# Six weight transposes of the first batch by DMA instead of TensorE, 512-key score matmuls, and new instruction orders in a post-norm decoder layer

## What is computed

```python
def attn(X):                                  # B=4, S=512, D=512, 16 heads
    Q, K, V = (X @ Wq.T + bq) * s, (X @ Wk.T + bk) * s, X @ Wv.T + bv
    scores = where(causal, einsum('bqhd,bkhd->bhqk', Q, K), -inf)
    return einsum('bhqk,bkhd->bqhd', softmax(scores), V) @ Wo.T + bo
def xattn(logits, ctx):                       # ctx: 4 x 512 x 256
    energy = (ctx @ Wxq.T + bxq) @ (ctx @ Wxk.T + bxk).T
    return einsum('bln,bmn->blm', logits, softmax(energy))
def ffn(x):
    xq = activation_quant(rms_norm(x))
    return (silu(xq @ sign(Wg).T) * (xq @ sign(Wu).T)) @ sign(Wd).T
x = layernorm(x + attn(x)); x = layernorm(x + xattn(x, ctx)); x = layernorm(x + ffn(x))
```

## Time and profile before

| | |
|---|---|
| median of 3 runs | 603.66 us (601.66 to 605.85) |
| the profiled execution | 603.64 us |
| its span from first to last instruction | 601.8 us |
| PE busy with matmuls | 562.8 us, 94% |
| DVE, ACT, POOL busy | 478.2, 431.5, 360.0 us |
| mean granted TensorE clock | 0.984 |

### The profile page before, as it was taken

One profiled execution on the slowest core, in us unless ns is written; L12 is line 12 of the kernel. 1 busy time (PEld: TensorE's weight loads), 2 busy tenths in 40 slices (PEclk: granted clock), 3 DMA queues, 4 the chain that ended last, 5 costly groups with the idle time before them and its releaser, 6 DMA issues.

```text
span 601.8 us, 14954 instructions
## 1 busy us (share of the span) xinstructions
PE 562.8 (94%) x5692; PEld 371.7 (62%) x5692; DVE 478.2 (79%) x1264; ACT 431.5 (72%) x813; POOL 360.0 (60%) x397
## 2 busy tenths in 40 slices
PE   5799799999979999999998989999999999999996
PEld 4457677686545664678645656676655666575572
DVE  5788879987878787788899767767879988768775
ACT  5799989874866987689776766754777987343351
POOL 1242321116763899669686758744779888655533
PEclk9999999999979999999999999999999999989999
DMA  9834885503354979987737739962287789731000
GB/s 327 303 99 113 221 211 166 160 2 88 71 106 86 205 149 169 184 160 160 139 72 131 117 103 162 166 120 48 75 155 133 155 167 172 132 106 36 19 36 35
DMA packets 199655, 79.10 MB, mean 131 GB/s; under 512 B 186144, under 2 KB 190752, under 8 KB 198048
## 3 DMA queue, kind: packets, MB, share of 16 engines
q1 hardware_dynamic: 199040, 77.62, 60.7%
q10 hardware_dynamic: 544, 0.52, 0.2%
HBM read 27.79 MB, written 4.19 MB: 53 GB/s over the span
## 4 chain that ended last, share of the span: by engine, by line
PE 51%; DVE 16%; POOL 10%; ACT 8%; DMA 6%; SPq 4%; issue 3%; POOLq 0%; DVEq 0%; ACTq 0%
PE ps_b L646 22%; PE ps_b L794 14%; PE ps_b L809 10%; POOL ph L1256 5%; DVE ps_b L1067 4%; SPq L588 2%; ACT p L891 2%; PE ps_b L738 2%; POOL hp L1252 2%; PE ps_b L717 2%; PE ps_b L702 2%; DMA pt<-ph 2%; DMA x1T<-rhl 2%; DMA bx<-in_b_x_dram 2%; DVE scaled L1157 1%
## 5 line engine op out<-in xcount | busy, mean ns | idle before, releaser
L1256 POOL TENSOR_TENSOR ph<-p,ph 128x768 f16<-128x768 f32 (+1 forms) x72 | 130.3, 1822 | 38.0 <-ACT ph L827 37.7
L891 ACT ACTIVATE p<-ps_b,tops 128x128 f32<-128x128 f32 (+3 forms) x256 | 121.2, 549 | 30.8 <-issue 18.4
L794 PE MATMUL ps_b<-xqT,sg 128*128 128x256 f16 x1024 | 121.1, 275 | 7.8 <-DVE o L1096 1.9
L1067 DVE CUSTOM_DVE_ANT_0 ps_b<-ps_b,future 128x128 f32<-128x128 f32 (+3 forms) x256 | 118.1, 519 | 11.1 <-PE ps_b L702 10.7
L809 PE MATMUL ps_b<-sd,hp 128*128 128x512 fp8e4 x512 | 117.7, 379 | 0.7 <-POOL hp L1252 0.6
L794 PEld LDWEIGHTS ps_b<-xqT,sg 128*128 128x128 fp8e4 x1024 | 99.1, 99 | 26.5 <-issue 4.9
L1252 POOL TENSOR_TENSOR hp<-gt,hp 128x512 f16<-128x512 f32 x64 | 73.9, 1161 | 61.1 <-ACT hp L827 60.9
L646 PE MATMUL ps_b<-xhl,wh 128*128 128x256 f16 x480 | 84.9, 277 | 0.5 <-DVE ks L1049 0.5
L809 PEld LDWEIGHTS ps_b<-sd,hp 128*128 128x128 f16 x512 | 48.4, 98 | 56.4 <-issue 2.0
L827 ACT ACTIVATE ph<-p 128x768 f16<-128x768 f32 (+1 forms) x72 | 65.4, 920 | 4.1 <-DMA pt<-ph 3.9
L646 PE MATMUL ps_b<-xhl,wl 128*128 128x256 f16 x240 | 66.5, 277 | 0.0
(11 more groups left out here) (115 smaller groups left out, 974.8 us busy)
## 6 DMA issues: line engine op xcount, KB each, us to landing
hp<-in_sgT_dram SPq DMA_DIRECT2D x6, 1024.0 KB, 5.5
gt<-in_sgT_dram SPq DMA_DIRECT2D x6, 1024.0 KB, 6.0
rows<-in_x_dram SPq DMA_DIRECT2D x8, 512.0 KB, 3.6
out_dram<-rows SPq DMA_DIRECT2D x16, 256.0 KB, 2.6
xin<-in_xT_dram SPq DMA_DIRECT2D x14, 256.0 KB, 3.3
e<-in_ctxT_dram SPq DMA_DIRECT2D x4, 512.0 KB, 4.5
pt<-ph SPq DMA_TRANSPOSE x72, 4.3
hp<-in_wT_dram SPq DMA_DIRECT2D x4, 256.0 KB, 4.8
```

What stands on the lines that cost most here:

```text
L794: ins = pe.matmul(ps[:, a * HALF:(a + 1) * HALF], sg[:, ("gg", "uu").index(name), c, ht * P:(ht + 1) * P], xqT[:, c, :], start=c == 0, sto ...
L891: ins = act.activation(p32[:, n % P32_SLOTS, to:to + keys], ps[:, col:col + keys], ACT.Exp, scale=-1.0, bias=tops[:, s % 2, g, j, qt % 2:q ...
L1067: ins = dve.tensor_tensor_reduce(scores, scores, future[:, S - width:S], EXP_SCALE, 3e38, ALU.add, ALU.min, tops[:, s % 2, g, j, qt % 2:qt ...
L1256: pool.tensor_tensor(out_, in_, hi, ALU.subtract).then_inc(signal, 1)
```

## The change

1. `FIRST` is replaced by a list: `BY_PE` names the 18 pairs that PE turns, all others go by DMA. Of the first batch these are pairs 13, 15, 17, 19, 21 and 23: the second pair (heads 2 and 3) of groups 1, 2 and 3, for i = 0 and for i = 1. Their high part is a copy made by DVE from `p` to `ph` (`HIGH_DVE`), the low part comes from POOL as for the later pairs, and SP starts the transposes.
2. `key_runs`: where the two halves' keys lie in neighbouring slots of `ks` (s = 1, 5 and 7) and the block has 512 keys (i = 0), one matmul covers both slots instead of two of 256.
3. All five orders and the bank numbers are new. `bi` moves ahead of two weight chunks, `sm` and `lc0` ahead of `lw3`.

```diff
-FIRST, SHARED = 24, 24
+ALL_PAIRS, SHARED = 96, 24
+BY_PE = (0, 1, 2, 3, 4, 5, 6, 7, 8, 9, 10, 11, 12, 14, 16, 18, 20, 22)
+BY_DMA = tuple(n for n in range(ALL_PAIRS) if n not in BY_PE)
+HIGH_DVE = tuple(n for n in BY_DMA if n < SHARED and n % 2)
+HIGH_ACT = tuple(n for n in BY_DMA if n not in HIGH_DVE)
...
+def key_runs(s, width):
+
+    if width == S and (s - 1) % K_SLOTS + 1 < K_SLOTS:
+        return ((0, S),)
+    return ((0, min(width, HALF)), *(((1, width - HALF),) if width > HALF else ()))
...
 SP_ORDER = """
-lw0.0 lw0.1 lw0.3 lw0.2 lw2.0 lw1.1 lw1.3 lw2.1 lw1.0 lw1.2 lw2.2 lw3 lw2.3 sm bi lc0 lx1 lg0 lg1 lr0 lr1 lg2 lg3 lx2
...
+lw0.0 lw0.1 lw0.3 lw0.2 lw2.0 lw1.1 lw1.3 lw2.1 lw1.0 bi lw1.2 lw2.2 sm lc0 lw3 lw2.3 lx1 lg0 lg1 lr0 lr1 lg2 lx2 lg3
...
             def turn_weights(s, g, i, pair):
                 n, blocks = pairs_to(s, g, i, pair), 4 * width_of(s, i) // P
-                wait(sp, p_lo, 0, n - FIRST + 1)
+                wait(sp, p_lo, 0, BY_DMA.index(n) + 1)
                 pt_free(sp, n)
...
                     for hq, hk in ((0, 0), (0, 1), (1, 0)):
-                        for kh in range((width + HALF - 1) // HALF):
-                            keys = min(width - kh * HALF, HALF)
+                        for kh, keys in key_runs(s, width):
...
-                                ins = pe.matmul(banks[j][:, col + kh * HALF:col + kh * HALF + keys],
+                                scores = banks[j][:, col + kh * HALF:col + kh * HALF + keys]
+                                ins = pe.matmul(scores.rearrange("p (h n) -> p h n", h=halves),
                                                 qs[mine, s % Q_SLOTS, g, hq, qt % 2 * P:(qt % 2 + 1) * P],
-                                                ks[mine, (s - h + kh) % K_SLOTS, g, hk, 0:keys],
+                                                ks[mine, slot:slot + halves, g, hk, 0:keys // halves],
...
                     n = pairs_to(s, g, (3 - qt) * h, j // 2)
-                    if n < FIRST:
-                        wait(pe, tw_lo, 0, 2 * n + 2)
+                    if n in BY_PE:
+                        wait(pe, tw_lo, 0, 2 * BY_PE.index(n) + 2)
                     else:
-                        wait(pe, turned[n % PT_SLOTS], (n - FIRST) // PT_SLOTS, 16)
+                        wait_turned(pe, n)
```

More of the change, by code:

```diff
@@ L260 @@
[L260 to L263 removed]
+k0 ws0.0 xs0.0.0 xs0.0.1 ws0.1 ws0.2 ws0.3 ws1.0 ws1.1 ws1.2 ws1.3 ws2.0 ws2.1 ws2.2 bv qk0.0.0 qk0.0.1 wx mx0.0.0.0
@@ L487, in freed_by @@
             if name == "tw":
-                return tw_lo, 0, 2 * pairs_to(s, *parts[:-1]) + parts[-1] + 1
+                return tw_lo, 0, 2 * BY_PE.index(pairs_to(s, *parts[:-1])) + parts[-1] + 1
             if name == "qk":
@@ L507, in ph_free, with wait_turned, ph_slot @@
         def ph_free(eng, n):
-            if n >= FIRST + PH_SLOTS:
-                wait(eng, turned[(n - PH_SLOTS) % PT_SLOTS], (n - FIRST - PH_SLOTS) // PT_SLOTS, 16)
+            rank = BY_DMA.index(n) - PH_SLOTS
+            if rank >= 0:
+                wait_turned(eng, BY_DMA[rank])
+        def wait_turned(eng, n):
+            before = sum(m % PT_SLOTS == n % PT_SLOTS for m in BY_DMA if m < n)
+            wait(eng, turned[n % PT_SLOTS], before, 16)
+        def ph_slot(n):
+            return BY_DMA.index(n) % PH_SLOTS
         def pt_free(eng, n):
@@ L884, in exponentials @@
                 before = n - P32_SLOTS
-                if 0 <= before < FIRST:
+                if before in BY_PE:
                     act.wait_ge(*filled("tw", *pair_at(before), 1))
-                elif before >= FIRST:
-                    wait(act, p_lo, 0, before - FIRST + 1)
+                elif before >= 0:
+                    wait(act, p_lo, 0, BY_DMA.index(before) + 1)
                 for qt, col, keys in tiles_of(s, i):
@@ L905, in p_high @@
                 ph_free(act, n)
-                split(ph[:, n % PH_SLOTS, 0:width], p32[:, n % P32_SLOTS, 0:width], p_hi[0].sem)
+                split(ph[:, ph_slot(n), 0:width], p32[:, n % P32_SLOTS, 0:width], p_hi[0].sem)
             def low_products(s, g):
@@ L1080, in turned_low @@
                 for j, cols, hi, lo in halves_of(n, width):
-                    wait(dve, tw_hi, 0, 2 * n + j + 1)
+                    wait(dve, tw_hi, 0, 2 * BY_PE.index(n) + j + 1)
                     ps = bank_of("tw", s, g, i, pair, j)
@@ L1263, in p_low @@
                 n, width = pairs_to(s, g, i, pair), 2 * width_of(s, i)
-                if n < SHARED:
-                    wait(pool, p_hi[pair], 0, (n - FIRST) // 2 + 1)
-                else:
-                    wait(pool, p_hi[0], 0, (SHARED - FIRST) // 2 + n - SHARED + 1)
-                hi, lo = (ph[:, n % PH_SLOTS, half * width:(half + 1) * width] for half in range(2))
+                if n in HIGH_DVE:
+                    wait(pool, p_hi[1], 0, HIGH_DVE.index(n) + 1)
+                else:
+                    wait(pool, p_hi[0], 0, HIGH_ACT.index(n) + 1)
+                hi, lo = (ph[:, ph_slot(n), half * width:(half + 1) * width] for half in range(2))
                 low(lo, p32[:, n % P32_SLOTS, 0:width], hi, p_lo.sem)
```

389 lines of the change are left out of this document (194 added, 195 removed).

## The result

The changed kernel takes 584.14 us (median of 4 runs, 582.25 to 585.39) against 602.66 us for the one before beside it (4 runs, 601.41 to 605.85): ratio 0.9674, 95% interval 0.9632 to 0.9717. The profiled execution has a span of 580.5 us, 21.3 less than before.

A forecast was written before the change was run, and what follows sets the result against it. PE was taken to bound the kernel, with 39 us of its span without a matmul, plus slow clock after waits. Terms -4.5 + 1.0 + 0 - 3.6 - 3.0 + 3.6 = -6.5 gave 597.1 us, range 588 to 606.

The forecast's parts named there:

- Transposes, -4.5: First batch, six pairs: 42 transposes taken from PE at 0.108 us each save 4.5 us.
- The dear transposes (9.2 us): Rival: the 42 removed transposes save 9.2 instead of 4.5 us, giving 592.4 us; chance 0.07.
- The late turn, +1.0: Last pair of the first batch: its DMA chain takes 11.6 us against 10.6 of PE cover, costing 1.0 us.
- The rival of 612 to 626 us: Rival: DMA turns come late behind loads or waiting instructions in SP's queue, stalling groups 1 to 3; chance 0.08.
- The 512 keys, 0: Score matmuls: twelve of 512 columns cost as much as 24 of 256, so no change.
- The start, -3.6: First place, group 1 scores and context projection: bank waits of 2.05 and 1.53 us go, saving 3.6 us.
- The third place, -3.0: Scores of group 3: half of 5.9 us, from 3.28 of waiting and 2.6 of clock, is saved.
- Unplaced new waits, +3.6: Anywhere in the five new orders: three new waits of the mean 1.2 us each add 3.6 us.
- The later batches, 0: The three later batches have the same tasks in slightly other places, so no change.
- The rival of ACT's relief: Rival: waits near 72 us and the slow clock behind them go too, giving 585.3 to 589 us; chance 0.12.
- The rival of waits that change place: Rival: waits PE loses in the scores come back in the next task, giving 603.7 us; chance 0.24.

The follow-up runs named there:

- e3: The changed kernel with its new orders, but the six pairs turned by TensorE again instead of by DMA: 589.07 us, ratio 0.9741 to the kernel before.
- a_again: The changed kernel itself, run once more without any change as a measure for a run beside it: 584.48 us, ratio 0.9673 to the kernel before.
- e2: The kernel before with its old orders, the six pairs turned by DMA and the 512-key matmuls put in: 610.06 us.
- e4: Old orders with the six DMA turns, the steps of pairs 19 and 23 moved earlier in the DVE, GpSimd and SP queues: 609.75 us.
- e1: The changed kernel with the 512-key score matmuls split again into two of 256 keys: ratio 0.9670 to the kernel before.
- h3: The kernel before with only the new start, up to 26 us, and the 512-key merge; all turns by TensorE: ratio 0.9976.
- e5: The kernel before, with DVE's evictions of three projections moved ahead of the quantisation of the second tile of rows: 601.61 us.
- e7: The kernel before, all orders kept, with each GpSimd low product of attention weights cut into four instructions: 608.06 us.
- h1: The changed kernel up to 176 us of its trace, then the old order of all five engines: 595.16 us.
- h2: Old orders and TensorE turns up to 174 us of the old trace, then the new order, with the 512-key merge: 606.97 us.
- h6: The changed kernel with the old order only behind 445 us of its trace: 590.25 us.
- h7: Old orders and TensorE turns up to 400 us of the old trace, then the new order, with the 512-key merge: 608.58 us.
- e6: The kernel before with three places of TensorE's order exchanged in the later batches: 601.66 us, ratio 0.9983.

## Why the prediction was wrong

By its own terms, lost time should have changed by -3.6 - 3.0 + 3.6 + 1.0 = -2.0 us; it changed by -16.2. The work, forecast at -4.5, changed by -5.1, of which the six pairs are 4.6 by the paces (4.1 to 4.6 us of time, e3 against a_again).

- **Transposes, -4.5: right.** Their pace of 0.108 us holds. The dear transposes (9.2 us) do not show. Neither does the figure of the Trainium skill ("TensorE: Matmul & The Clock Gate", Part 4: PE-mode transpose), about 275 ns for a transpose in a kernel; the estimate by it would be 11.6 us.
- **The late turn, +1.0: absent**, in the new orders, although the six turns took 3.7 to 9.5 us to land there, with a median of 5.6, more than the 4.3 that I took. I had worked out the cover of the last pair, but the place of each step in its queue decides: with the same turns in the old orders PE waits 6.8 us for them (e2), and one that goes out right behind two loads of 1 MB takes 10.1 (e4). The rival of 612 to 626 us was near for another kernel than the one built (e2, 610.06 us).
- **The 512 keys, 0: right** (e1).
- **The start, -3.6: right in size** (3.7 us at 30 us), but it does not stay by itself, as I had taken for granted. Alone it is given back by 60 us (h3); it stays in the changed kernel, whose order goes on behind it.
- **The third place, -3.0: too small.** Between 150 and 180 us the lost time fell from 8.5 to 3.9, by 4.6. I had put the wait down to DVE's order alone. It had two causes that had to come together, for taking away either removes the wait but for 0.47 us at most: the order (e5) and DVE's instructions standing under GpSimd's (e7).
- **Unplaced new waits, +3.6: the first step that failed.** PE's waits got no such addition: beyond the first it stands idle for 29.4 - 5.9 = 23.5 us against 39.0 - 6.3 = 32.7. I drew them from the mean of the old waits, as if the new orders were the old ones disturbed. They are a whole of their own. What I priced there is true of a splice: h1, h2, h6 and h7 pay 4 to 8 us at theirs.
- **The later batches, 0: the step that cost most.** "The same tasks in slightly other places" lost 8.1 us less, some 4.6 of them by their order (7.7 less by a_again). The order's rows there, which bank a product takes and what had just filled it, I had not compared.

Together: 8.1 for the later batches, 4.6 for two additions that did not come, 1.6 for the third place make 14.3, and 14.2 were missing; each share is open to the 2.5 us by which two traces differ. The rival of ACT's relief gave 585.3 to 589 us and came nearest, by a mechanism that didn't act: its waits near 72 us did not go. From 60 to 80 us PE waits 3.1 us, 2.4 of them for ACT in one piece, against 3.3 before. The rival of waits that change place holds in the main for the single exchanges (h3, e5, e6), and not for the whole.

## What to carry to other kernels

Where five queues in fixed order feed one another, a wait taken away in one place mostly came back here a few microseconds later, and a splice into the order cost more than most single gains; so an edit that rewrites the whole order is not the sum of its local edits, and its later parts must be read as closely as its first. Compare lost time at fixed points, not totals: that showed where an order was better even in kernels that came out slower. Look at what filled a bank last before a product takes it, and at what GpSimd runs while DVE is on the path.

## What the runs showed of the hardware

DVE's instructions of the quantising, from SBUF to SBUF with f32 input (`scaled`, `xq`), take 0.49 and 0.43 us alone and up to 1.96 under one of GpSimd's products. In the trace of before eleven of 32 take over 0.7 us, each lies under GpSimd work for at least four fifths of its length, and each ends 0.28 us behind the end of a GpSimd product of 512 columns or more. Under GpSimd's instructions of one column they stay at 0.43 to 0.51. With GpSimd's products in four pieces four of over 0.7 us are left (e7). The Trainium skill ("SBUF — State Buffer", SBUF: two separate sides) says that the two share a pair of ports by an exclusive lock that is held for a whole instruction, so that the loser stands still; this case's traces agree: of the three products in 5.21 us the first two end at 165.96 and 167.75 us, and `scaled` and `xq` end at 166.25 and 168.03, each just behind one of them, however short it is alone. I had read these 1.96 us in the old trace as a quantising that is simply long.
